# Attention scores from two float32r parts on quarters of the array, with the long attentions' value products taken four key tiles at a time

## The reference

```python
x = x + _L0_xattn_ref(_layernorm(x), ctx_1024, mask_BxS2_bk0, ...)   # 6404 keys, masked       "cross0"
x = x + _L0_ffn_ref(_layernorm(x), ...)                              # self attention, 1024     "self0", then experts
x = x + _L1_xattn_ref(_layernorm(x), ctx_1024, ...)                  # causal self attention    "self1"
                                                                     # 6404 keys, not masked    "cross1", then a dense block
x = x + _L1_ffn_ref(_layernorm(x), ...)                              # experts

def _mha(q_in, k_in, v_in, Wq, Wk, Wv, bv, causal):
    ...
    scores = jnp.einsum('bhse,bhte->bhst', q, k) * scale
    p = jax.nn.softmax(scores, axis=-1)
    o = jnp.einsum('bhst,bhte->bhse', p, v)
```

## Time and profile before

| what | us |
|---|---|
| median of 3 runs | 2640.31 (2638.06 to 2641.78) |
| span of the profiled execution | 2636.5 |
| PE busy | 2357.0 |
| DVE busy | 2344.4 |
| ACT busy | 2132.2 |
| POOL busy | 282.7 |

### The profile page before, as it was taken

The page is one execution under the profiler, slowest core; times in us unless marked ns, Lnnn a source line. Parts: engine busy times, 40 slices in busy tenths (PEclk is TensorE's granted clock), DMA queues, the critical chain, the costliest instruction groups (busy, mean ns, idle before and its releaser), DMA issues.

```text
span 2636.5 us, 59029 instructions
## 1 busy us (share of the span) xinstructions
PE 2357.0 (89%) x23035; PEld 739.1 (28%) x23035; DVE 2344.4 (89%) x2657; ACT 2132.2 (81%) x4065; POOL 282.7 (11%) x836
## 2 busy tenths in 40 slices
PE   4899999999999999589768869999999999999986
PEld 2322222222222222122332232222222222222224
DVE  4999999999999998599747689999999999999935
ACT  3599999999999998369716728999999999999971
POOL 3200110101000001200003400000000100000000
PEclk7899999999999999789978979999999999999998
DMA  6011111111101101211121220111111111111000
GB/s 189 25 38 44 44 33 44 46 41 35 31 30 30 38 25 38 95 48 43 38 69 47 63 74 18 39 34 30 30 31 38 37 31 31 30 35 38 8 3 9
DMA packets 73354, 108.74 MB, mean 41 GB/s; under 512 B 13301, under 2 KB 53986, under 8 KB 73082
## 3 DMA queue, kind: packets, MB, share of 16 engines
q1 hardware_dynamic: 67786, 98.21, 12.1%
q0 software_dynamic: 2032, 3.61, 0.8%
q10 hardware_dynamic: 3264, 3.15, 0.4%
HBM read 72.69 MB, written 23.48 MB: 36 GB/s over the span
## 4 chain that ended last, share of the span: by engine, by line
PE 72%; DVE 16%; ACT 5%; issue 3%; DMA 1%; SPq 1%; POOL 1%; ACTq 0%; DVEq 0%
PE ps L1645 71%; DVE maxima L1388 13%; ACT probs L1174 3%; ACT probs L1131 1%; DVE maxima L1328 1%; PE ps L1651 0%; POOL probs L897 0%; DVE stats L1264 0%; DMA k_cross<-probs 0%; DVE z L1258 0%; DMA k_self<-probs 0%; DVE z L1280 0%; SPq L709 0%; DMA q_stages<-q_cross 0%; SPq L543 0%
## 5 line engine op out<-in xcount | busy, mean ns | idle before, releaser
L1388 DVE TENSOR_REDUCE maxima<-ps 128x1 f32<-128x920 f32 x1792 | 1889.8, 1110 | 64.4 <-PE ps L1645 64.2
L1174 ACT ACTIVATE probs<-ps 128x512 f32<-128x512 f32 (+1 forms) x3264 | 1762.5, 594 | 141.7 <-PE ps L1645 141.5
L1645 PE MATMUL ps<-probs,v_stage 128*16 128x256 f32 x14208 | 1158.0, 393 | 1.0 <-issue 0.3
L1645 PE MATMUL ps<-k_stages,q_stages 64*128 64x460 bf16 (+2 forms) x4032 | 753.9, 372 | 138.5 <-DVE maxima L1388 62.2
L1645 PE MATMUL ps<-q_stages,k_stages 64*128 64x512 bf16 (+1 forms) x3712 | 724.8, 380 | 41.2 <-ACT probs L1131 17.5
L1645 PEld LDWEIGHTS ps<-k_stages,q_stages 64*128 64x128 bf16 x4032 | 193.5, 93 | 996.5 <-issue 522.7
L1645 PEld LDWEIGHTS ps<-probs,v_stage 128*16 128x16 f32 x14208 | 236.9, 94 | 416.8 <-issue 361.8
L1328 DVE TENSOR_REDUCE maxima<-ps 128x2 f32<-128x1024 f32 (+1 forms) x224 | 239.9, 1106 | 67.5 <-PE ps L1645 64.3
L1131 ACT ACTIVATE probs<-ps 128x512 f32<-128x512 f32 x448 | 224.2, 554 | 50.3 <-PE ps L1645 48.6
L1645 PEld LDWEIGHTS ps<-q_stages,k_stages 64*128 64x128 bf16 x3712 | 187.5, 93 | 270.6 <-ACT probs L1174 69.6
L903 POOL COPY v_stage<-by_key 128x400 f32<-128x400 f32 x64 | 33.1, 518 | 948.1 <-PE ps L1645 869.4
(11 more groups left out here) (238 smaller groups left out, 882.2 us busy)
## 6 DMA issues: line engine op xcount, KB each, us to landing
q_stages<-q_cross SPq DMA_DIRECT2D x256, 48.0 KB
k_stages<-k_cross SPq DMA_DIRECT2D x64, 150.2 KB
k_stages<-k_cross SPq DMA_DIRECT2D x64, 150.0 KB
scratch<-acc_out SPq DMA_DIRECT2D x496, 16.0 KB
k_stages<-k_cross SPq DMA_DIRECT2D x64, 100.1 KB
k_stages<-k_cross SPq DMA_DIRECT2D x64, 100.0 KB
q_stages<-q_self SPq DMA_DIRECT2D x60, 96.0 KB
k_cross<-probs SPq DMA_DIRECT2D x12, 384.0 KB, 3.8
```

The lines of the kernel that those rows point to most:

```text
L1174: return nc.scalar.activation(probs[0:m, probs_slot(a, j, i), :], ps[0:m, b_bank(a, use), :], ACT.Exp, scale=float(E) ** -0.5)
L1388: nc.vector.tensor_reduce(maxima[:, at, seg:seg + 1], ps[:, A_BANK + 2 * (g % 2):A_BANK + 2 * (g % 2) + 2, 0:a.segment], AX_XY, ALU.max).t ...
L1645: return nc.tensor.matmul(out_, lhsT, rhs, start=start, stop=stop)
```

## The change

Every part is now a float32 number that is rounded to float32r, and two parts are enough: three terms, 24 rows, two rows for the maximum and one for the mask. 27 rows fit a quarter of the array's rows. `pass_a` stands on rows 0 to 31 and 64 to 95 (one for each side), `pass_b` on rows 32 to 63 and 96 to 127, so that the four products of a step are on four separate quarters. Keys and queries are staged once for `pass_a` and once for `pass_b`; keys have two slots in place of four. The third part's work on POOL goes away, and ACT's second part with it (DVE makes the second). In the long attentions `values_step` does all 512 columns of a batch at every second step.

```diff
-Q_PARTS = (0, 0, 0, 1, 1, 2)
-K_PARTS = (0, 1, 2, 0, 1, 0)
+PARTS = 2
+Q_PARTS = (0, 0, 1)
+K_PARTS = (0, 1, 0)
 TERMS = len(Q_PARTS)
 ROW_MAX = TERMS * E
-ROW_MASK = ROW_MAX + 3
+ROW_MASK = ROW_MAX + PARTS
+GROUP = 32
...
-    a.ring, a.sides = 4, 2
+    a.ring, a.k_ring, a.sides = 4, 2, 2
...
+        def a_row(side):
+            return side * SIDE
+        def b_row(side):
+            return side * SIDE + GROUP
...
-            def split(a):
-                for i, (kind, c0, n) in enumerate(a.jobs):
-                    b = i % a.splits
-                    pool.wait_ge(sem("split_part2"), a.jobs_before + i + 1)
-                    nc.gpsimd.tensor_tensor(a.parts[:, b, 2, 0:n], a.rest[:, b, 0:n], a.parts[:, b, 1, 0:n],
-                                            ALU.subtract).then_inc(sem("split_part3"), 1)
...
-                    link(nc.gpsimd.tensor_copy(parts[:, 0, :], neg))
-                    link(nc.gpsimd.tensor_tensor(rest, neg, parts[:, 0, :], ALU.subtract))
-                    link(nc.gpsimd.tensor_copy(parts[:, 1, :], rest))
-                    nc.gpsimd.tensor_tensor(parts[:, 2, :], rest, parts[:, 1, :],
+                    link(nc.gpsimd.tensor_copy(parts[:, 0, :].bitcast(F32R), neg))
+                    nc.gpsimd.tensor_tensor(parts[:, 1, :].bitcast(F32R), neg, parts[:, 0, :],
                                             ALU.subtract).then_inc(sem(a.name + "_max_parts"), 1)
...
                         last = mm(ps[:, A_BANK + 2 * (g % 2) + side, 0:a.segment],
-                                  qa_stage[rows, slot, qt * P:(qt + 1) * P], k_stage(a, slot)[rows, c:c + a.segment])
+                                  q_stages[rows, j % a.ring, qt * P:(qt + 1) * P].bitcast(F32R),
+                                  k_stage(a, j % a.k_ring)[rows, c:c + a.segment].bitcast(F32R))
...
-                        rows = slice(side * SIDE, (side + 1) * SIDE)
-                        mm(ps[:, b_bank(a, tile_use(a, j, i)), :], k_stage(a, slot)[rows, col:col + P],
-                           qb_stage[rows, slot, 0:BANK]).then_inc(sem(a.name + "_scores"), 1)
+                        rows = slice(b_row(side), b_row(side) + a.rows_b)
+                        mm(ps[:, b_bank(a, tile_use(a, j, i)), :],
+                           k_stage(a, j % a.k_ring)[rows, col:col + P].bitcast(F32R),
+                           q_stages[rows, j % a.ring, 0:BANK].bitcast(F32R)).then_inc(sem(a.name + "_scores"), 1)
...
-                    half, last = BANK // 2, 2 * (a.batches - 1)
-                    if p < last:
-                        values(j, p // 2, p % 2 * half, (p % 2 + 1) * half)
-                    elif p == last:
+                    last = 2 * (a.batches - 1)
+                    if p == last or p < last and p % 2 == 1:
                         values(j, p // 2, 0, BANK)
```

More of the change, by code:

```diff
@@ L25 @@
 F32 = mybir.dt.float32
+F32R = mybir.dt.float32r
 BF16 = mybir.dt.bfloat16
@@ L408, in transformer, with staged @@
         block = ctx.enter_context(nc.Block())
[L413 to L423 removed]
+        def staged(a, part, i):
+            return sem(f"{part}_staged_{i % a.k_ring}")
         def staged_before(a, slot):
[L427 to L428 removed]
+            return sum(b.stagings // b.k_ring * b.stage_dmas for b in attentions[:attentions.index(a)]
+                       if slot < b.k_ring)
         def staged_count(a, i):
[L432 to L433 removed]
+            return (staged_before(a, i % a.k_ring) + (i // a.k_ring + 1) * a.stage_dmas) * DMA
         def tile_use(a, j, i):
@@ L479, in q_rest_count @@
         def q_rest_count(a):
-            return (1 + (a is self1)) * 2 * a.sides * DMA
+            return (1 + (a is self1)) * a.sides * DMA
         def contexts_at(i):
@@ L623, in stage_keys, with stage_queries @@
                         row += parts * E
+            def stage_queries(a, part, j):
+                h, half = a.passes[j]
+                slot, done = j % a.ring, staged(a, part, j)
+                if j % H == 0 and part == "a":
+                    wait_stored(sp, a, a.q_at[half], a.q_at[half] + 1)
+                for side in range(a.sides):
+                    row = a_row(side) if part == "a" else b_row(side)
+                    sp.dma_start(q_stages[row:row + ROW_MAX, slot, 0:BANK],
+                                 a.q_dram[:, h * E:(h + 1) * E, half * BANK:(half + 1) * BANK]).then_inc(done, DMA)
             def store_early(e):
                 _, c0, n = EARLY[e]
-                sp.wait_ge(sem("early_part3"), e + 1)
+                sp.wait_ge(sem("early_split"), e + 1)
                 sp.dma_start(cross1.k_dram[:, :, c0:c0 + n].rearrange("a p c -> p a c"),
@@ L712, in stage_rest @@
                 def stage_rest():
                     wait_stored(sp, a, len(a.jobs) - 1, len(a.jobs))
-                    for side in range(a.sides):
-                        h, base = side, side * SIDE
-                        sp.dma_start(qa_stage[base:base + ROW_MAX, 0, BANK:N],
+                    for h in range(a.sides):
+                        row = b_row(h)
+                        sp.dma_start(q_stages[row:row + ROW_MAX, 0, :],
+                                     a.q_dram[:, h * E:(h + 1) * E, :]).then_inc(staged(a, "b", 0), DMA)
@@ L718, in stage_rest @@
+                    for h in range(a.sides):
+                        row = a_row(h)
+                        sp.dma_start(q_stages[row:row + ROW_MAX, 0, BANK:N],
                                      a.q_dram[:, h * E:(h + 1) * E, BANK:N]).then_inc(sem("q_rest"), DMA)
-                        sp.dma_start(qb_stage[base:base + ROW_MAX, 0, :],
-                                     a.q_dram[:, h * E:(h + 1) * E, :]).then_inc(sem("q_rest"), DMA)
                 def put_maxima(j):
@@ L1032, in _ @@
                     short_attention(a)
-                if a is cross0:
-                    clear_queries()
         @block.scalar
```

294 lines of the change are left out of this document (118 added, 176 removed).

## The result

The changed kernel takes 4,225.7 us in the median of 4 runs (4,203.5 to 4,255.1), the kernel before 2,641.1 beside it; the ratio is 1.601, 95% interval 1.594 to 1.608. The profiled execution has a span of 4,217.0 us, 1,580.5 more than before. The forecast was 2,874 us, with 2,730 to 3,030 as the range. The direction was right, the size was not.

A forecast was written before the change was run, and what follows sets the result against it. The prediction took a 1.07 us loop through ACT between pass_b products as the bound, with DVE and ACT nearly as tight. 2640.3 + 246 (long attentions) - 12 (elsewhere) = 2874 us; range for 8 in 10: 2730 to 3030.

The forecast's parts named there:

- The loop: Long attentions: PE waits for ACT to free a bank, so two pass_b stand at least 1.07 us apart.
- the rhythm: Long attentions: steps alternate, 1.12 us waiting for ACT and 1.37 with a whole batch; 704 pairs, +246 us.
- The faster rival: Whole kernel: PE's total work is the bound, so the change gains; about 2551 or 2625 us; chance 9%.
- The quarters' gap: Long attentions' steps: on separate quarters the gap from pass_a to pass_b shrinks from 0.21 us to 0.03.
- float32r: Score products: streams at the bf16 rate in one pass; a slower rate, about 3170 or 3790 us, had chance 5%.
- the weight load: float32r score products: between bf16's 93 ns and float32's 191, costed at 0.05 us extra at two places a pair.
- The clock: Rival: PE streams less, the clock falls to 1.2 GHz, whole batches take 0.86 us more, +600 and over; 5% with late staging.
- late staging: Rival: transfers come late, 4 us in each pass, +250 us; chance 5% together with a falling clock.
- Ahead of the attentions and in the short ones: Outside the long attentions: -7.5 us ahead of the attentions and -5 in self0's steps, sum -12; at best -25.
- Staging: SP's transfers in cross0's passes: 22 a pass in place of 20, two more at 0.7 us, costed at nothing.
- the cover that I named: Staging in a pass: over 5 us between score reads and turning of maxima, enough for six issues at 0.7 us.

The follow-up runs named there:

- the last run: Changed kernel plus zero-weight products over 128 rows, four groups ahead of the scores of each pass's first and seventh step: 3,902.7 us, ratio 1.478.
- the halves' run with lots at the first and seventh step: Changed kernel with 256-column values at every step, plus four groups of zero-weight 128-row products before each pass's first and seventh step's scores: 3,257.4 us, ratio 1.233.
- the rhythm run: Kernel before, bfloat16 on 64 rows a side, with only the long attentions' values done whole at every second step: 2,950.8 us, ratio 1.118.

## Why the prediction was wrong, step by step

**The loop and the rhythm: right.** At the clock of 1.00, in the last run, DVE waits for PE once a pair (0.47 us), ACT once (0.34, where about 0.3 was forecast) and PE once for ACT, and the whole batch alone costs 310 us where its rows had 303. The faster rival, that PE's total decides, is out: PE has fewer products and the time goes up even where the clock holds.

**The quarters' gap: right.** 0.03 was chosen between 0 and 0.21; it is 0.01 at both levels (605.31 to 605.32, 383.73 to 383.74).

**float32r: right about one pass, the weight load at the far end.** Groups of weight loads by form, from 400 to 424 us of the halves' run with lots at the first and seventh step, all at 1.00:

```profile
L1601 PEld LDWEIGHTS ps<-q_stages,k_stages 27*128 27x128 f32 x36 | 3.3, 181 | 0.8 <-issue 0.4 <-ACT probs L1138 0.2
```

181 ns, next to float32's 191 and not to bfloat16's 93; I had taken the middle. A product's record is 0.50 us in place of 0.38. Both make the loop 1.18 to 1.20 where 1.12 was forecast, and the step with the batch 1.41 where 1.37 was; the pair 2.61 in place of 2.49. At the upper clock the sum would have been 704 x (2.61 - 2.14) = 331 in place of 246, about 2,960 us with the rest of the forecast, and in its range. That is worked out, not run.

**The clock: the step that failed.** It stood among the rivals, in the 5% shared with late staging, at "+600 and over". The argument against it was the last pass of cross1, at 1.00 with less for PE to do. That row was read for PE's work alone. Its products stand on 64 rows; the change puts 27 in their place, and no row of before has such products. The diff names them, and I costed what it did to the time of a product and never asked what it did to the clock. The reason that the rival was given, that PE streams less, is not the one that the runs show: with PE's waits and 64 rows the clock is 0.948, and with 27 rows and PE busy for 99% it is 0.50. The price was low as well: I put 0.86 us on each whole batch only, and at 0.50 every product of a step is longer. The pair is 4.04 against 2.61, 1.43 x 704 = 1,007 us; the rhythm and float32r make 331 of the excess. A pass is 23.0 us longer (53.0 against 30.0), 1,472 us in 64 passes; these two terms leave 134 us of it, 2.1 a pass, for the steps at its start, where I had left 5.77 us as they were.

**Ahead of the attentions and in the short ones: wrong, mostly by the same step.** -12 was forecast. From the second result of self0 to some 2 us after SP begins to stage cross1's keys, before and after:

```profile
1165.00:1517.00 352.00, 285.49 (x2569) 97.67 (x2565) 259.52 (x386) 238.85 (x501) 69.84 (x272) 0.90 0.17 51
```

```profile
1904.00:2348.00 444.00, 369.57 (x2573) 137.72 (x2569) 265.68 (x386) 239.51 (x496) 55.36 (x212) 0.70 0.14 46
```

92 us more for the same work of DVE and ACT, at 0.70 in place of 0.90. That is most of the 108 us which the 64 passes leave of the 1,580.5; self1's wait in the next point is a part of it. Ahead of the four attentions, from the last score product of one to the first of the next (from the span's start for cross0), the changes are +4.1, -1.0, +0.6 and -2.2 us for cross0, self0, self1 and cross1: some +1.5 together, where -7.5 was forecast.

**Staging: nothing in the long attentions, not so in the short ones.** PE waits for the maxima's transfers 40.4 us in the whole run, before it was 2.9. Nearly all of it is at the first pass of self0 and of self1 (timeline of the first; self1's wait is 19.64 us):

```profile
1858.90 21.97 SPq L729 DMA_DIRECT2D q_stages<-max_rows  x4
...
1873.12 0.79 PE L1599 MATMUL ps<-q_stages,k_stages 26*128 26x512 f32 x2 [16.11 <-DMA q_stages<-max_rows]
```

SP issues the maxima of this pass at 1858.90, and PE's wait for them ends at 1873.12, 14.2 us later. Before, they were issued at 1136.60, and the pass_b that needs them ran at 1140.38, 3.8 us later and without a wait. Ahead of them in SP's order stand the stagings of the pairs: in the stretch from 1,820 to 1,880 us 16 transfers of keys in place of 8 before, and their data flow at 75 to 79 GB/s from 1,845 us until 1,872, some 1 us before the wait ends; that the maxima queue behind this data is argued from these rows and was not tried alone. I had counted the transfers of cross0 only. At most some 37 us of the 108 are this. In the long attentions PE waits for the maxima at their very starts alone (2.40 and 2.25 us); with halves at 1.00, where passes are shorter, the wait of 1.27 us in the trace above is of this kind, so the cover that I named is thin.

**What stays open.** That rows alone suffice to hold the clock down is shown in the kernel (bfloat16, 27 rows). What makes it fall once it is up is shown less well: each of the 147 falls in cross0, in seven runs' traces, stands at most 2.5 us behind a wait of 0.45 us or more, and the stretches without waits had none, but the same waits often pass without a fall, and no run of the attentions took the waits away without adding products over 128 rows. How much of the changed kernel's own low clock is the rows and how much the type is not: on four quarters bfloat16 rose and float32r did not, and no kernel was run with float32r over 64 rows in the attentions. Why one of two like passes of the last run fell and the other did not, I can't say.

## What to carry to other kernels

A change that puts a product on fewer rows of the array, and more so if it lets PE wait more often, is to be asked what it does to the granted clock before anything is priced at the old one; where no row of the trace has such products, the case at half the clock is a rival with a real chance, and its price is every product on PE's path. If the clock has fallen, look for the wait after which it fell and for what PE does from there on: a few products over all rows, put behind the waits rather than ahead of them, gave 330 us here, in a kernel that was still 23% slower than the one before. And a shorter total for an engine is worth nothing where a loop through another engine sets the distance of the steps.

## What the runs showed of the hardware

- A clock of 0.50 under a full load: PE busy for 99% of 400 us in bfloat16 over 27 rows a product, without a rise.
- Keeping and winning are two things: float32r products on quarters kept 1.00 for 110 steps behind wide products, and stayed at 0.50 for 110 steps behind a standstill.
- float32r at 1.00: weight load 181 ns for 128 columns (bfloat16 93, float32 191), product record 0.50 us for 512 columns (0.38 in bfloat16), and a step of four score products and a half batch, without waits, 0.99 us on four quarters and 1.19 on two sides where bfloat16 takes 0.88 and 1.07.
- The clock can fall under 64-row products too, but there it came back by itself: eight falls between 170 and 1,100 us of the rhythm run, each over within 4 us.
